# A Flamingo-style block on one core: in its 1444-key attention, the key, value and left-maximum products are cut into two 64-row products placed among the scores, and the bank ring becomes two banks and one apart

## The reference

```python
def _split_heads(x):
    B, S, _ = x.shape
    return x.reshape(B, S, N_HEADS, HEAD_DIM).transpose(0, 2, 1, 3)
qm = _split_heads(q @ Wq.T + bq)
km = _split_heads(k @ Wk.T + bk)
vm = _split_heads(v @ Wv.T + bv)
scores = jnp.einsum('bnlh,bnph->bnlp', qm, km) / np.sqrt(HEAD_DIM).astype(np.float32)
mask = attention_mask[:, None, None, :]
scores = jnp.where(mask, scores, MASK_FILL)
attn = jax.nn.softmax(scores, axis=-1)
out = jnp.einsum('bnlp,bnph->bnlh', attn, vm)
B, _, L, _ = out.shape
out = out.transpose(0, 2, 1, 3).reshape(B, L, D_MODEL)
return out @ Wo.T + bo
```

## Time and profile before

| | us |
|---|---|
| median of 3 runs | 2200.03 |
| the profiled execution | 2202.07 |
| its span, first to last instruction | 2200.1 |
| PE busy / DVE / ACT / POOL | 1933.5 / 1515.2 / 1310.9 / 582.4 |
| ACT's waits for scores, whole run | 292.8 |
| DVE's waits for maximum products, whole run | 154.7 |

### The profile page before, as it was taken

The page is one execution under the profiler, slowest core; times in us unless marked ns, Lnnn a source line. Parts: engine busy times, 40 slices in busy tenths (PEclk is TensorE's granted clock), DMA queues, the critical chain, the costliest instruction groups (busy, mean ns, idle before and its releaser), DMA issues. The chain is left out here.

```text
span 2200.1 us, 42925 instructions
## 1 busy us (share of the span) xinstructions
PE 1933.5 (88%) x16790; PEld 1295.2 (59%) x16790; DVE 1515.2 (69%) x3603; ACT 1310.9 (60%) x2169; POOL 582.4 (26%) x525
## 2 busy tenths in 40 slices
PE   3769999666799999999999999999987887878997
PEld 2536676444466666666666666666654555555554
DVE  4845666795678888888888888888824666664554
ACT  3636667685166666666766667667753554453444
POOL 1410223312523132223214223222203224220122
PEclk9879999777599999999999999999975787788999
DMA  5025555002223233233233223323302002002340
GB/s 155 1 73 184 184 171 173 14 27 72 92 75 124 86 108 129 81 108 129 80 113 126 99 94 125 112 97 124 116 10 61 15 22 43 1 22 41 68 85 29
DMA packets 125141, 190.74 MB, mean 87 GB/s; under 512 B 41890, under 2 KB 99338, under 8 KB 123534
## 3 DMA queue, kind: packets, MB, share of 16 engines
q1 hardware_dynamic: 124942, 188.01, 27.6%
HBM read 104.84 MB, written 11.76 MB: 53 GB/s over the span
## 5 line engine op out<-in xcount | busy, mean ns | idle before, releaser
L1615 DVE TENSOR_REDUCE b_part_max<-psum 128x1 f32<-128x482 f32 (+3 forms) x1248 | 739.6, 649 | 199.4 <-PE psum L1504 154.7
L1419 ACT ACTIVATE b_PT<-psum 128x800 f32<-128x800 f32 x768 | 601.7, 835 | 295.6 <-PE psum L1523 292.8
L1523 PE MATMUL psum<-b_QS,b_KS 64*128 64x200 f32 x3072 | 452.7, 291 | 6.7 <-ACT b_PT L1419 6.6
L1504 PE MATMUL psum<-b_KH,b_QBD 64*128 64x482 f32 (+1 forms) x1152 | 432.9, 449 | 12.5 <-POOL b_QBL L1330 11.1
L1523 PEld LDWEIGHTS psum<-b_QS,b_KS 64*128 64x128 f32 x3072 | 360.9, 189 | 13.5 <-ACT b_PT L1419 8.2
L1504 PEld LDWEIGHTS psum<-b_KH,b_QBD 64*128 64x128 f32 x1152 | 202.7, 189 | 198.6 <-DVE b_part_max L1615 135.2
L1539 PE MATMUL psum<-b_PT,b_V 128*32 128x200 f32 x6144 | 306.0, 340 | 0.1
L1351 POOL TENSOR_TENSOR b_KL<-b_KF,b_KH 128x1444 fp32r<-128x1444 f32 x32 | 106.1, 3314 | 741.4 <-ACT b_KH L1393 741.4
L1539 PEld LDWEIGHTS psum<-b_PT,b_V 128*32 128x32 f32 x6144 | 180.8, 110 | 71.4 <-ACT b_PT L1419 0.8
L1901 ACT ACTIVATE c_HE<-psum,C 128x400 f32<-128x400 f32 x128 | 75.7, 595 | 94.6 <-PE psum L2117 90.1
L419 POOL TENSOR_TENSOR a_rs<-a_ve,a_half 100x4 f32<-100x4 f32 x48 | 48.6, 1012 | 312.4 <-DVE a_ve L911 312.3
(11 more groups left out here) (278 smaller groups left out, 3040.8 us busy)
## 6 DMA issues: line engine op xcount, KB each, us to landing
b_KS<-b_KH SPq DMA_DIRECT2D x64, 722.0 KB
a_CT<-in_ctxt SPq DMA_DIRECT2D x32, 722.0 KB, 5.8
b_CT<-in_ctxt SPq DMA_DIRECT2D x32, 722.0 KB, 4.2
b_KS<-b_KL SPq DMA_DIRECT2D x32, 722.0 KB
a_CN<-in_ctxn SPq DMA_DIRECT2D x32, 704.0 KB
att_scratch<-b_AO SPq DMA_DIRECT2D x32, 200.0 KB, 5.7
c_G<-gates_scratch SPq DMA_DIRECT2D x4, 1600.0 KB
c_KBD<-gates_scratch SPq DMA_DIRECT2D x4, 1600.0 KB
```

What stands on the lines that cost most here:

```text
L1419: nc.scalar.activation(PT[:, kt % 3, 2 * a:2 * a + 2, :], psum[:, 2 * a:2 * a + 2, 0:TG], ACT.Exp).then_inc(sem["pt_ready"], 1)
L1504: m = mm(bank(b, D, size), QBD[rows, j % 2, tile * D:(tile + 1) * D], KH[rows, j % 2, at_:at_ + size], start=True, stop=True)
L1523: m = mm(bank(p, D, 2 * T, (s % 2) * 2 * T), KS[rows, j % 2, s, kt * D:(kt + 1) * D], QS[rows, j % 2, s * 2 * T:(s + 1) * 2 * T], start=Tr ...
L1615: v.tensor_reduce(part_max[0:rows, q, c:c + 1], bank(b, rows, CHUNKS[c][1]), AX.X, ALU.max)\
```

## The change

Jobs get places between single scores. Positions 0 to 7 of a tile stand before its scores 0 to 7, `GAP` before the weighting, `AFTER` behind it. The three maxima of an even tile are all of half 0, at positions 0, 3 and 6, those of an odd tile of half 1, at 2, 5 and `GAP`. A value job becomes 8 products with 64 rows: four of half 1 beside the even tile's scores 0 to 3, four of half 0 beside the odd tile's scores 4 to 7; a key job becomes 4 (two column halves in each row half) at positions 1, 2 of its tile and 5, 7 of the next; a left job becomes 2, at position 7 of an even tile and 1 of the next, with `QBL` widened to 128 columns by zeros. The two row halves of a job add up in one bank, and the second waits for the first by `half_filled`. Keys and values have bank 7 (`SIDE`) for themselves; maxima, lefts, queries and turns share banks 4 and 5. Queries (now 4 products of 32 columns each) and the turn (tile 7) stand behind the weighting. `CT` and `QBL` get a cleared rest; the stage's first jobs stay whole.

```diff
-RING = (4, 5, 7)
+RING, SIDE = (4, 5), 7
...
-PHASES = 5
+GAP, AFTER = 8, 9
...
-VALUE_SLOTS, LEFT_SLOTS, KEY_SLOTS = (0, 2, 6), (0, 2, 6), (4, 8, 10)
-TURN_SLOT = 8
+QUERY_SLOTS = (((0, 1), (1, 3), (2, 5), (3, 9)), ((4, 1), (5, 9)), ((6, 1),), ())
+VALUE_SLOTS, LEFT_SLOTS, KEY_SLOTS = (0, 2, 6), (0, 2, 4), (4, 8, 10)
+TURN_SLOT = 7
+FIRST_MAX = TURN_SLOT + 1
+EVEN_POS, ODD_POS = (0, 3, 6), (2, 5, GAP)
...
+    mains = []
+    for step in range(KT):
+        kt = (FIRST_MAX + step) % KT
+        for k, pos in enumerate(ODD_POS if kt % 2 else EVEN_POS):
+            c, tile = divmod(step // 2 * 3 + k, TILES_ROW)
+            mains.append((kt % 2, tile, c, kt, pos))
...
+    for i, (_, _, _, kt, pos) in enumerate(MAINS):
...
+            jobs.append((kt, pos, 0, (g, j + 2, "max", i), None))
         if i >= EARLY and nxt:
...
+            jobs.append((kt, pos, 0, (g, j + 1, "max", i), None))
     if not last:
...
+        jobs += [(kt, AFTER, 1, (g + 1, 0, "query", r), None) for r, kt in QUERY_SLOTS[j]]
     if nxt:
...
+        for r, kt in enumerate(VALUE_SLOTS):
+            jobs += [(kt, k, 1, (g, j + 1, "value", r), k) for k in range(4)]
+            jobs += [(kt + 1, 4 + k, 1, (g, j + 1, "value", r), 4 + k) for k in range(4)]
+        for c, kt in enumerate(LEFT_SLOTS):
+            jobs += [(kt, 7, 1, (g, j + 1, "max", len(MAINS) + c), 0), (kt + 1, 1, 1, (g, j + 1, "max", len(MAINS) + c), 1)]
+        jobs.append((TURN_SLOT, AFTER, 0, (g, j + 1, "turn", 0), None))
     if after:
...
+        for r, kt in enumerate(KEY_SLOTS):
+            jobs += [(kt, 1 + k, 1, (g, j + 2, "key", r), k) for k in range(2)]
+            jobs += [(kt + 1, 5 + 2 * k, 1, (g, j + 2, "key", r), 2 + k) for k in range(2)]
...
-        QBL = sb("QBL", [D, 2, 2 * LEFT], F32R)
+        QBL = sb("QBL", [D, 2, D], F32R)
...
+            def ring_bank(what):
+
+                r = ring_no[what]
+                if r >= len(RING):
+                    pe.wait_ge(sem["ring_drained"], r - len(RING) + 1)
+                return RING[r % len(RING)]
...
+            def half_key(what, part):
+
+                g, j, _, i = what
+                half, k = (1, part) if part < 2 else (0, part - 2)
+                if part == 0:
+                    side_free(what)
+                    keys_loaded(g, j, i)
+                if part == 2:
+                    pe.wait_ge(sem["half_filled"], half_no[what])
+                rows = slice(ROW * half, ROW * half + ROW)
+                c, size = CHUNKS[i]
+                c, size = c + k * (size // 2), size // 2
+                m = mm(bank(SIDE, D, size, k * size), w("xkT")[rows, :], CT[rows, j % 2, c:c + size], start=part == 0, stop=part == 3,
+                       skip_group_check=True)
+                if part == 1:
+                    half_no[what] = len(half_no) + 1
+                    m.then_inc(sem["half_filled"], 1)
+                if part == 3:
+                    m.then_inc(sem["key_filled"], 1)
+
...
+            def half_value(what, part):
+
+                g, j, _, i = what
+                half, k = (1, part) if part < 4 else (0, part - 4)
+                if part == 0:
+                    side_free(what)
+                if part == 4:
+                    pe.wait_ge(sem["half_filled"], half_no[what])
+                rows = slice(ROW * half, ROW * half + ROW)
+                at = (4 * i + k) * D
+                m = mm(bank(SIDE, D, D, k * D), CT[rows, j % 2, at:at + D], w("xvT")[rows, :], start=part == 0, stop=part == 7,
+                       skip_group_check=True)
+                if part == 3:
+                    half_no[what] = len(half_no) + 1
+                    m.then_inc(sem["half_filled"], 1)
+                if part == 7:
+                    m.then_inc(sem["v_filled"], 1)
+
...
+            def half_left(what, half):
+
+                g, j, _, i = what
+                if half == 0:
+                    half_no[what] = len(half_no) + 1
+                    b = ring_bank(what)
+                else:
+                    b = RING[ring_no[what] % len(RING)]
+                    pe.wait_ge(sem["half_filled"], half_no[what])
+                at, size = CHUNKS[max_tile(i)[2]]
+                rows = slice(ROW * half, ROW * half + ROW)
+                m = mm(bank(b, D, size), QBL[rows, j % 2, :], KH[rows, j % 2, at:at + size], start=half == 0, stop=half == 1,
+                       skip_group_check=True)
+                m.then_inc(sem["ring_filled" if half else "half_filled"], 1)
...
+            def score(g, j, kt, q):
 
                 n = g * GROUP + j
+                p, s = divmod(q, 2)
...
-                if a == 0:
+                if q % 4 == 0:
                     wait(pe, sem["pt_ready"], n * 2 * KT + (2 * kt + half - 1))
...
+                s += 2 * a
+                m = mm(bank(p, D, 2 * T, (s % 2) * 2 * T), KS[rows, j % 2, s, kt * D:(kt + 1) * D],
+                       QS[rows, j % 2, s * 2 * T:(s + 1) * 2 * T], start=True, stop=True)
+                if q % 4 == 3:
                     m.then_inc(sem["st_psum"], 1)
...
+                    jobs = slot_jobs(g, j, last)
+
+                    def some(kt, pos):
+                        for at_kt, at_pos, _, what, part in jobs:
+                            if (at_kt, at_pos) == (kt, pos):
+                                job(what, part)
...
-                        for p in range(4):
-                            some(PHASES * kt + p)
+                        for q in range(8):
+                            some(kt, q)
                             if not last or ahead[0] < GROUP:
-                                score_piece(g, *ahead, p)
-                        some(PHASES * kt + 4)
+                                score(g, *ahead, q)
+                        some(kt, GAP)
                         if kt % 2:
                             weigh(g, j, kt - 1)
                             weigh(g, j, kt)
-
-            for i, what in enumerate(first_ring_jobs()):
-                job(i, 0, *what)
...
+                if kind == "key":
+                    dve.wait_ge(sem["key_filled"], key_no[g, j, kind, i] + 1)
+                    if i == 0:
+                        dve.wait_ge(t.mask_loaded[p], (2 * g + (j // 2 + 1)) * 16)
+                        wait(dve, sem["kl_ready"], n)
+                    c, size = CHUNKS[i]
+                    v.scalar_tensor_tensor(out=KF[:, c:c + size], in0=bank(SIDE, D, size), scalar=col("xk"),
+                                           in1=MB[:, p, c:c + size], op0=ALU.add, op1=ALU.mult).then_inc(sem["key_drained"], 1)
```

More of the change, by code:

```diff
@@ L1429, in slots @@
                     n = g * GROUP + j
-                    keys, highs = find(g, j, last, "key"), find(g, j, last, "value")
                     for kt in range(KT):
@@ new lines, in side_free, with query @@
+            def side_free(what):
+                if what in side_before:
+                    before = side_before[what]
+                    if before[2] == "value":
+                        pe.wait_ge(sem["v_drained"], value_no[before] + 1)
+                    else:
+                        pe.wait_ge(sem["key_drained"], key_no[before] + 1)
+            half_no = {}
+            def query(what):
+                g, j, _, i = what
+                b = ring_bank(what)
+                if i == 0:
+                    pe.wait_ge(sem["ht_loaded"], (g + (j // GROUP + 1)) * 16)
+                for r in range(4):
@@ new lines, in maximum @@
+            def maximum(what):
+                g, j, _, i = what
+                b = ring_bank(what)
+                half, tile, c = max_tile(i)
+                if tile == 0:
+                    pe.wait_ge(sem["kh_ready"], 3 * (g * GROUP + j) + c + 1)
+                if i == 0:
+                    pe.wait_ge(sem["qbd_ready"], g * GROUP + j + 1)
+                at, size = CHUNKS[c]
+                rows = slice(ROW * half, ROW * half + ROW)
+                mm(bank(b, D, size), QBD[rows, j % 2, tile * D:(tile + 1) * D], KH[rows, j % 2, at:at + size],
+                   start=True, stop=True).then_inc(sem["ring_filled"], 1)
@@ L1483, in job, with turn @@
+            def turn(what):
+                g, j, _, _ = what
+                b = ring_bank(what)
+                pe.wait_ge(sem["mx_ready"], g * GROUP + j + 1)
+                nc.tensor.transpose(bank(b, QCH, D), mx[:, 0:QCH], t.ident).then_inc(sem["ring_filled"], 1)
+            def job(what, part):
+                kind = what[2]
+                if kind == "query":
+                    query(what)
+                elif kind == "turn":
+                    turn(what)
                 elif kind == "key":
-                    if i == 0:
-                        pe.wait_ge(t.ct_loaded[j % 2], (2 * g + (j // 2 + 1)) * 16)
@@ L1564, in slots @@
                             weigh(g, j, kt)
-            for i, what in enumerate(first_ring_jobs()):
-                job(i, 0, *what)
+                        some(kt, AFTER)
```

(16 more changed lines are left out.)

199 lines of the change are left out of this document (79 added, 120 removed).

## The result

The changed kernel takes 2325.16 us (median of 4 runs, 2321.41 to 2335.11), the kernel before 2201.56 us beside it: ratio 1.0543, 95% interval [1.0506, 1.0579]. It is slower by some 120 us, inside the range 2245 to 2345 and 37 us above the 2288 foreseen. The profiled execution took 2321.41 us (span 2319.4).

The account below looks back on a forecast made before the run. It took PE and DVE as coupled through the banks between them, neither free. From 2202 us, 83 for 30 samples and 5 for the start gave 2290, less the profiled run's 2.04 us excess: 2288 us, range 2245 to 2345.

Parts of the forecast that it names:

- the sum: Attention stage: 2.76 us more per sample without queries, times 30 samples 83 us, plus 5 us at the stage's start.
- Left pairs, 6.02 us: Pair of key tiles with a left product: 6.02 us, against 5.27 before, or 5.02 for one now sharing a key's pair.
- the walk: Step-by-step timing of one pair's products, drains and exponentials through two banks, giving 6.02 us with a left, 5.27 without.
- lefts that hold scores: Left halves waiting for a bank hold up the scores behind them; without this the sum falls 40 us, to 2248.
- Pairs without a left, 5.27 us: Pair of key tiles without a left product: last maximum loads at 3.36, plus 0.41 and 1.50, gives 5.27 us.
- one product per 0.61 us: Two ring banks, each use taking 1.22 us, pass one product per 0.61 us, just above DVE's 0.57.
- Maximum 3 takes the bank free at 1.79: Pair without a left: the fourth maximum loads 1.79 us after the first, as soon as its bank is free.
- Pieces hidden: Value and key half products run beside the other half's scores at no cost; open price 1.8 and 2.0 us per job.
- The rival of strict order: Scores wait for the half product ahead of them across row halves: +1.7 us x 30, about 2340 us, chance 0.06.
- The signs named: If right: longer PE waits for b_part_max and exponential waits for scores, DVE less busy, no 128-row product in mid pair.
- The query at no difference: Query products moved behind the weighting cost nothing more or less, having PE for themselves before and after.
- The start, 5 us: Stage's start: 51 maxima through two banks at 0.61, up to 0.71 us at slower clock: 2 to 7, taken as 5.

Follow-up runs that it names:

- run 1: Changed kernel with the left product whole again (one 128-row product before the weighting), all else as changed: 2273.71 us, ratio 1.0321 to the kernel before.
- Run 8: Changed kernel with DVE's maximum taken over only the first half of each product's columns, PE's products all there: 2272.94 us, ratio 1.0308 to the kernel before.
- run 9: Against run 5, only the maxima moved to the changed kernel's places and halves: 2263.25 us, ratio 1.0240 to the kernel before.
- run 10: Run 9 with maxima at the same scores but on the half these scores do not use: 2201.81 us, ratio 0.9955 to the kernel before.
- run 7: Against run 5, values and keys cut into 64-row halves within one even tile, sharing three banks: 2406.39 us, ratio 1.0907 to the kernel before.
- run 3: Changed kernel with values, keys and lefts all whole again, still two ring banks and bank 7 apart: 2405.19 us, ratio 1.0892 to the kernel before.
- run 4: Run 3 with values and keys sharing a ring of three banks (4, 5, 7) with the maxima, same order: 2253.75 us, ratio 1.0195 to the kernel before.
- run 6: Changed kernel, every product cut and placed as there, but banks 4, 5 and 7 shared as one ring: 2314.21 us, ratio 1.0485 to the kernel before.
- run 5: Against run 4, maxima (but one), lefts and turn back in their old places, queries still behind the weighting: 2197.27 us, ratio 0.9957 to the kernel before.

## Why the prediction was right, and where it was off

- **The sign and the size.** The span grew by 119.3 us where the sum had 88. The 31 us come from: 18.7 between first and last output copy (101.7 against 83), 11.9 in the stage's start, and 0.8 from the stages around it (6.9 later at the stage's start, 6.1 less after its last copy; this start lay anywhere from 536.3 to 549.4 us in the thirteen profiles).
- **Left pairs, 6.02 us.** Shown: 6.03, 6.04 and 6.16 us, with the steps of the walk met within 0.03 us in the pair above, and runs 1 and 8 take the two causes away one by one (the second half in the same bank; the length of a drain). The prediction priced lefts that hold scores at 40 us; the cut of the lefts cost 49.
- **Pairs without a left, 5.27 us, and "one product per 0.61 us".** 5.38 to 5.42 us (5.87 with the turn, against 5.83), and the cause was wrong. The step that failed: "Maximum 3 takes the bank free at 1.79". Maximum 3 stands behind the odd tile's first scores, and these wait for the even tile's first exponential; I timed only the second there. The first comes late since the maxima at scores 0 and 3 went to half 0, the half of these scores; my only price for a maximum among scores of its half was "0.2 us of columns", once, at maximum 4. Run 8 shows that the banks don't bind here, runs 9 and 10 that the half delays the exponential and costs 62 us. That 5.27 was only 0.11 to 0.15 us short is luck: the chain that I walked was not the one that bound the pair.
- **Pieces hidden.** In the changed kernel, yes: its first exponentials start 1.20 and 1.23 us after the pair, run 9's without pieces 1.17. But that rests on where the maxima are. I had let "each row half run its own queue"; run 7 shows that it doesn't. The rival of strict order is refuted as stated, for in run 7 a score passes one piece. Its sign, scores 0.22 us apart beside value pieces, does stand in the changed kernel's weight loads (1028.48 and 1028.70), but it comes from the maximum in the scores' own half: the first score's product starts 0.32 us after that maximum's there, and 0.34 us after it in run 9, where no piece stands near. The changed kernel, then run 9:

```profile
1028.38 0.48 PE L1562 MATMUL psum<-b_KH,b_QBD 64*128 64x482 f32 x1
...
1028.70 0.25 PE L1624 MATMUL psum<-b_QS,b_KS 64*128 64x200 f32 x1
...
1017.86 0.49 PE L1574 MATMUL psum<-b_KH,b_QBD 64*128 64x482 f32 x1
1018.20 0.57 PE L1636 MATMUL psum<-b_QS,b_KS 64*128 64x200 f32 x5
```

  The Trainium skill, "TensorE: Matmul & The Clock Gate", part 3 on row and column tiling, lets matmuls start strictly in program order. Run 7's rows disagree, with a score's product at 1042.95 us and that of the piece ahead of it at 1043.27, yet the halves aren't free of each other either.
- **The signs named.** DVE is less busy and no 128-row product stands in mid pair, as said. Wrong: PE's waits for `b_part_max` fell, to 31.2 and 33.1 us, and the exponentials' waits for scores did not grow (235.9 us against 256.1). Most of the waiting goes to the scores, which wait for exponentials (61.8 + 38.7 us): the mark of the late first exponential more than of the banks.
- **Banks.** 151 us between runs 3 and 4 for whole products. For cut ones a third bank is worth nothing in the steady part (run 6): by the order of the jobs a cut product keeps one through both tiles of each pair.
- **The query at no difference.** Four samples have 144.04 - 4 x 34.89 = 4.5 us of query cost, 130.84 - 4 x 31.68 = 4.1 before: right within 0.1 us per sample.
- **The start, 5 us.** Mis-sized: 16.9 us (115.5 from stage start to first copy, 98.6 before). DVE's maxima and then two of three key drains there:

```profile
575.17 1.23 DVE L1719 TENSOR_REDUCE b_part_max<-psum 128x1 f32<-128x482 f32 x2 [0.29 <-PE psum L1562]
576.69 1.23 DVE L1719 TENSOR_REDUCE b_part_max<-psum 128x1 f32<-128x482 f32 x2 [0.29 <-PE psum L1562]
...
606.06 0.72 DVE L1696 SCALAR_TENSOR_TENSOR b_KF<-psum,C,b_MB 128x482 f32<-128x482 f32 x1 [0.99 <-PE psum L1502]
608.85 0.72 DVE L1696 SCALAR_TENSOR_TENSOR b_KF<-psum,C,b_MB 128x482 f32<-128x482 f32 x1 [2.07 <-PE psum L1502]
```

  Two maxima take 1.52 us, 0.76 each against 0.57, more than my upper end of 0.71: 51 x 0.19 = 9.7 us. The keys follow each other by 2.79 us since one bank serves them all, which I had not counted. The rows of the kernel before:

```profile
592.35 0.72 DVE L1608 SCALAR_TENSOR_TENSOR b_KF<-psum,C,b_MB 128x482 f32<-128x482 f32 x1 [1.00 <-PE psum L1487]
593.95 1.55 DVE L1608 SCALAR_TENSOR_TENSOR b_KF<-psum,C,b_MB 128x482 f32<-128x482 f32 x2 [0.89 <-PE psum L1487]
```

- **The clock.** 1.00 in the steady part, as foreseen; in the start it stays at its lower level (0.50, 1.2 GHz) longer. The changed kernel from 620 to 630 us, then the kernel before from 610 to 620:

```profile
620.00:630.00 10.00, 9.69 (x73) 7.67 (x76) 5.62 (x9) 5.11 (x7) 0.00 (x0) 0.50 0.40 136
...
610.00:620.00 10.00, 9.79 (x119) 6.92 (x115) 8.07 (x15) 6.64 (x10) 0.00 (x0) 1.00 0.01 2
```

  The kernel before has 1.00 from 610 us on; its stage began 6.9 us earlier. What the clock alone costs no run took apart.

## What to carry to other kernels

A cut that fills idle rows is paid where its partial sums live: price the bank that it holds from first piece to last drain, and what takes turns in the banks left, before the array's time. Where two row halves share the array, put a job on the half that the critical scores around it don't use, and time the first consumer of each pair (here the first exponential), not only the bank that comes free next. Of a change in several parts, run each alone: here a small gain (run 5, 0.43%) was hidden under three losses: the maxima's halves, the cut lefts, and a cut of values and keys that pays less than the bank it takes. The forecast's sum left out the first.
